# A step pipeline of hyperbolic attention: the chain from vector addition to feed-forward drawn together, its wide products on other steps

## The chip, the cores and the metric

One core of a Trainium2 chip runs the whole program. The time is device microseconds (us) of one execution; engines are PE (TensorE), DVE (VectorE), ACT (ScalarE), POOL (GpSimd) and SP, which issues the DMAs here.

## The reference, cut to what matters

The program is four blocks in a row on x of 8 samples, 512 rows, 256 columns, all in float32: a mixture of experts with a recurrent attention, a transformer block on the Poincaré ball, and two layers of windowed attention. The change touches the second alone. In this block `logmap0`, `expmap0` and `plin` scale each row by a function of its norm:

```python
ada = t_emb @ w_ada + b_ada
sh_msa, sc_msa, g_msa, sh_mlp, sc_mlp, g_mlp = jnp.split(ada, 6, axis=-1)
residual = x
xn = layer_norm(logmap0(x))
xm = expmap0(xn * (1 + sc_msa) + sh_msa)
...
attn = jax.nn.softmax(scores, axis=-1)
out_h = expmap0(jnp.einsum('bhqk,bhkd->bhqd', attn, vt))
attn_out = plin(_from_heads(out_h), w_o, b_o)
attn_t = g_msa * logmap0(attn_out)
x = mobius_add(residual, expmap0(attn_t))
residual = x
xn = layer_norm(logmap0(x))
xm = expmap0(xn * (1 + sc_mlp) + sh_mlp)
ff = plin(plin(xm, w_f1, b_f1), w_f2, b_f2)
ff_t = g_mlp * logmap0(ff)
return mobius_add(residual, expmap0(ff_t))
```

D is 256, there are 16 heads of 16, and the feed-forward is 1024 wide. `mobius_add` is the vector addition of the title.

## The kernel before, in words

`ball_parts` writes the block as a pipeline of numbered steps G. Each engine has a function `step(G)` that issues its share of step G, and each engine runs its steps in order; between the engines there are only semaphores. A sample has S = 16 attention steps (4 groups of heads times 4 key tiles), sample b those from 16b to 16b + 15, and everything else of a sample stands at a fixed distance from 16b: `at(G, 24)` gives the sample b with G = 16b + 24. What is due at distance a falls into the attention steps of a later sample, at phase a mod 16. A period is 16 steps; "phase 8" means the steps with G mod 16 = 8.

One step on PE is: the scores of step G + 1 (L1793), the side jobs of this step, the values of step G (L1806). ACT takes the exponentials of step G + 1 first (L1250, L1251, two halves of 1024 columns), then its other jobs. The scores use one set of four PSUM banks, so that those of G + 2 wait for the exponentials of G + 1.

The side jobs put their products into a ring of three PSUM banks (`RING`, `claim`, `place`): a job takes the bank that the job three places ahead of it had, and waits until ACT or DVE has emptied that one. The order of the ring is that of the jobs in the program. The jobs, with those who empty them:

- every fourth step: "ur" (the turned rows of the next sample's tile, L1848, emptied by ACT), phases 3, 7, 11, 15; "qk" and "v" (L1857, emptied on DVE by `projected`, L1449) and "pk" (row sums of the softmax, L1816, emptied by `invert`, L1503, at the end of the DVE step), phases 0, 4, 8, 12; "bc" (reciprocals spread, L1823, emptied by `divide`, L1514, near the start of the DVE step after), phases 1, 5, 9, 13; "zq" and "zk" (heads turned, L1841, emptied by ACT L1310 and by `keys`, L1493), phases 2, 6, 10, 14;
- once a sample: "wo0", "wo1" (product with w_o, L1832, emptied by `update` at the step after and by squares on ACT, L1269 to L1273), distances 18, 19; "fu0", "fu1" (rows of the feed-forward turned, L1865); "f0" to "f7" (first product of the feed-forward, two a step by the table `F1`, L1876, emptied by `hidden`, L1650); "fn" (norms, L1883); "y0" to "y3" (second product by `F2`, L1892, emptied one step later, `YS`, by `output_rows`, L1666).

On DVE the chain of a sample after its attention is: `update`, `step_limit`, `step_length`, `step_factors` (the first Möbius addition's factors), `applied` (L1564, the rows after ACT has scaled them in `scaled_rows`, L1326), `row_norms` (L1575), `row_angles` (seventeen operations on 128x4 and a root asked from POOL, L1217), `row_variances` (after a logarithm on ACT, L1354), `row_scales`, `rows2` (four tiles, into `u2`, which lies on the same memory as `fsq`, the squares of the hidden rows, so that it waits for POOL's sums of the sample ahead, `acc_ok`), `ask_rows2`, `limit_rows2`, then on ACT `scaled_rows2` and on PE "fu". A second chain of the same kind follows the outputs: `step_limit`, `step_length`, `step_factors`, `scaled_update` (ACT), `result`. `ask_heads` (L1457 and sixteen operations more) stands in phases 1, 5, 9 and 13, at the end of the DVE step, `limit_heads` (L1030 to L1484) at the start of phases 0, 4, 8 and 12.

The last sample has its attention in steps 112 to 127. All that comes after step 127 has no attention beside it; I call it the tail. The windowed layers are a block of their own and load their rows after the last result is stored.

## Time and profile before

| | us |
|---|---|
| median of 3 runs (lowest, highest) | 3677.0 (3676.5, 3677.7) |
| profiled execution, its own time | 3681.4 |
| its span | 3679.6 |
| PE busy in the span | 3405.7 (93%) |
| DVE busy | 2207.2 (60%) |
| ACT busy | 1698.4 (46%) |
| POOL busy | 383.3 (10%) |
| scores of step 0 of the ball block to scores of step 127 | 1230.5 to 2006.9 |
| scores of step 127 to the start of the windowed block | 2006.9 to 2155.0 |

Busy time says where an engine had work, not who waited: in this block the start of each group of scores on PE dates the steps, and the rows further down are windows cut at those starts. PE's clock is given there as a share of 2.4 GHz: 1.00 is 2.4 GHz, and 0.5 is 1.2 GHz.

### The profile page before, as it was taken

What the parts mean: (1) busy time and instruction counts of PE and PEld (TensorE: products, weight loads), DVE (VectorE), ACT (ScalarE), POOL (GpSimd) and SP (SyncE); (2) the same over time, 40 slices, a digit from 0 to 9 for tenths busy, and PEclk for the clock granted to TensorE, in tenths of its full rate; (3) what the DMA queues carried; (4) which work ended last, traced back from release to release, by engine and by line L of the source; (5) the groups of instructions that cost most, each with busy time, mean ns of one, the idle gap of its engine ahead of it and who ended that gap; (6) DMA issues with size and microseconds to landing.
All of it is one profiled execution on the core that took longest, in us unless ns stands there. A gap on an engine that the chain in (4) does not pass through costs nothing. (4 is left out here: it accounts for less than half of the span.)

```text
span 3679.6 us, 51595 instructions
## 1 busy us (share of the span) xinstructions
PE 3405.7 (93%) x18082; PEld 1915.6 (52%) x18082; DVE 2207.2 (60%) x6620; ACT 1698.4 (46%) x3271; POOL 383.3 (10%) x250
## 2 busy tenths in 40 slices
PE   8999999999996788998899758999999999999999
PEld 3455555555554333444444435555555555555554
DVE  3243343343357567778775648777777777777773
ACT  2233333333342455555556325555555555555552
POOL 0000000000000001111211211111111111111110
PEclk8999999999998799999999879999999999999999
DMA  4110120110000200000000030000000000000000
GB/s 175 53 61 32 35 72 32 35 61 32 29 15 13 76 5 8 7 15 14 11 12 12 9 131 21 20 21 21 21 21 21 21 27 21 26 27 27 21 27 20
DMA packets 77985, 120.47 MB, mean 33 GB/s; under 512 B 10224, under 2 KB 66315, under 8 KB 72608
## 3 DMA queue, kind: packets, MB, share of 16 engines
q1 hardware_dynamic: 77728, 117.17, 9.4%
q8 instruction: 146, 2.39, 0.3%
q14 instruction: 111, 0.91, 0.1%
HBM read 96.13 MB, written 16.83 MB: 31 GB/s over the span
## 5 line engine op out<-in xcount | busy, mean ns | idle before, releaser
L2616 PE MATMUL wps<-w_wqkv,w_hT 128*128 128x512 f32 x768 | 379.2, 618 | 3.1 <-DMA w_wo<-in_wwo 3.1
L2654 PE MATMUL wps<-w_xnT,w_w 128*128 128x512 f32 (+1 forms) x768 | 352.5, 599 | 24.5 <-DVE w_xnT L2479 20.3
L2238 POOL TENSOR_TENSOR w_rn<-w_n,w_mhalf 128x16 f32<-128x16 f32 x64 | 187.3, 2926 | 1097.7 <-DVE w_n L2416 1097.7
L2266 ACT ACTIVATE w_pr<-w_sm,w_nmx,w_rn 128x256 f32<-128x256 f32 (+1 forms) x512 | 286.5, 562 | 10.0 <-DVE w_nmx L2397 9.4
L1217 POOL TENSOR_TENSOR b_routs<-b_rins,b_expo 128x4 f32<-128x4 f32 x88 | 89.8, 1023 | 1839.0 <-DVE b_rins L1405 1839.0
L2654 PEld LDWEIGHTS wps<-w_xnT,w_w 128*128 128x128 f32 (+1 forms) x768 | 133.6, 179 | 217.9 <-issue 194.3
L656 PE MATMUL ps<-xT,b_late 128*128 128x512 f32 x512 | 245.8, 602 | 0.0
L672 PE MATMUL ps<-hid,b_late 128*128 128x512 f32 x512 | 240.8, 592 | 0.0
L1250 ACT ACTIVATE bb_pr<-ps 128x1024 f32<-128x1024 f32 x128 | 130.6, 1020 | 198.6 <-PE ps L1793 197.7
L2253 ACT ACTIVATE w_pT<-wps 128x512 f32<-128x512 f32 (+1 forms) x128 | 69.6, 544 | 329.7 <-PE wps L2563 329.7
L2616 PEld LDWEIGHTS wps<-w_wqkv,w_hT 128*128 128x128 f32 x768 | 138.2, 193 | 132.8 <-issue 127.8
L2666 PE MATMUL wps<-w_w,w_h2T 128*128 128x256 f32 (+1 forms) x768 | 190.1, 392 | 1.8 <-issue 1.8
L298 ACT ACTIVATE hid<-ps,rb 128x512 f32<-128x512 f32 x128 | 87.9, 687 | 222.6 <-PE ps L656 222.4
L2392 DVE CUSTOM_DVE_ANT_0 w_sm<-wps,w_wmask 128x256 f32<-128x256 f32 (+1 forms) x512 | 168.9, 386 | 34.8 <-issue 33.6
L2666 PEld LDWEIGHTS wps<-w_w,w_h2T 128*128 128x128 f32 (+1 forms) x768 | 137.4, 189 | 61.9 <-issue 48.6
L1876 PE MATMUL ps<-bb_uT,bb_wf 128*128 128x512 f32 x256 | 139.1, 689 | 31.8 <-DVE bb_fT L1650 14.4
L672 PEld LDWEIGHTS ps<-hid,b_late 128*128 128x128 f32 x512 | 97.1, 190 | 121.9 <-issue 121.5
L510 DVE TENSOR_REDUCE mx<-ps 128x8 f32<-128x512 f32 x32 | 22.1, 691 | 217.4 <-PE ps L753 217.4
L2275 ACT ACTIVATE w_qkr<-wps 128x512 f32<-128x512 f32 x128 | 76.4, 597 | 157.9 <-PE wps L2616 157.4
L2563 PEld LDWEIGHTS wps<-w_ident,w_pr 128*128 128x128 f32 x896 | 101.7, 142 | 77.0 <-issue 52.1
L407 DVE TENSOR_TENSOR hid<-hid,wm 128x512 f32<-128x512 f32 x128 | 88.3, 691 | 88.7 <-ACT hid L298 87.7
L2407 DVE TENSOR_SCALAR w_pr<-w_pr,w_ri 128x256 f32<-128x256 f32 (+1 forms) x512 | 137.6, 332 | 4.5
(329 smaller groups left out, 6680.4 us busy)
## 6 DMA issues: line engine op xcount, KB each, us to landing
b_late<-in_ew SPq DMA_DIRECT2D x32, 1024.0 KB, 6.7
w_xa<-xs SPq DMA_DIRECT2D x16, 512.0 KB, 3.9
w_xin<-xs SPq DMA_DIRECT2D x64, 128.0 KB, 3.8
xT<-in_xT SPq DMA_DIRECT2D x8, 512.0 KB, 3.8
xres<-in_x SPq DMA_DIRECT2D x32, 128.0 KB, 2.2
x<-x1t SPq DMA_DIRECT2D x32, 128.0 KB, 1.7
b_mod<-ada SPq DMA_DIRECT2D x16, 256.0 KB, 3.2
xs<-bb_wb SPq DMA_DIRECT2D x8, 512.0 KB, 2.9
```

The costliest lines, as they stand in the source:

```text
L656: ins = te.matmul(ps[:, G % 2], w1[:, k, j % M1 * P:(j % M1 + 1) * P], xT[:, b % 2, k], start=(k == 0), stop=(k == KD - 1))
L672: ins = te.matmul(ps[:, 2 + c], w2[:, j % M1, c * P:(c + 1) * P], hid[:, G % 4], start=(j == 0), stop=(j == J - 1))
L1250: a.activation(pr[:, G % 2, 0:2], ps[:, SC:SC + 2], ACT.Exp, scale=DH ** -0.5).then_inc(p_ok, 1)
L1876: ins = te.matmul(to, wf1[:, k, m * P:(m + 1) * P], uT2[:, k], start=(k == 0), stop=(k == KD - 1))
L2238: g.tensor_tensor(rn[:, i % 2, t], n2[:, n % 2, 1], mhalf[:], ALU.pow).then_inc(nr_ok, 1)
L2266: ins = a.activation(pr[:, j, lo:], sm[:, j, lo:], ACT.Exp, bias=nmx[:, G % 2, j:j + 1], scale=rn[:, i % 2, t, h:h + 1], accum_out=rs[:, G ...
L2392: ins = v.tensor_tensor_reduce(out=sm[:, j, lo:], in0=ps[:, g, c2 * 256 + lo:c2 * 256 + 256], in1=wmask[:, lo:], scale=1.0, scalar=-3.0e38 ...
L2407: ins = v.tensor_scalar(pr[:, j, lo:], pr[:, j, lo:], ri[:, G % 2, j:j + 1], None, ALU.mult)
L2563: ins = te.transpose(ps[:, 2 + g, (2 * c2 + k) * P:(2 * c2 + k + 1) * P], pr[:, j, k * P:(k + 1) * P], ident[:])
L2616: ins = te.matmul(to, hT[:, i % 2, k, t * P:(t + 1) * P], wqkv[:, i // B, k, s * 512:(s + 1) * 512], start=(k == 0), stop=(k == KD - 1))
L2654: ins = te.matmul(to[0:n], w1[:, i // B, k, lo:lo + n], xnT[:, k], start=(k == 0), stop=(k == KD - 1))
L2666: ins = te.matmul(to[:, a * D:(a + 1) * D], h2T[0:n, m, t * P:(t + 1) * P], w2[0:n, i // B, m], start=(m == 0), stop=(m == MH - 1))
```

## The change

Only distances and places within a step are changed; no operation is added or removed. By distance from 16b:

| job | before | after |
|---|---|---|
| first addition: `scaled_rows` (ACT), `applied` and `row_norms` | 24, 25 | 23, 24 |
| `row_angles` | 26 | 24, late in the DVE step |
| logarithm, `row_variances`, `row_scales` | 26, 27, 28 | 25, 25, 26 |
| `rows2` | 28, 29 | 26, 27 |
| `ask_rows2`, `limit_rows2`, `scaled_rows2`, "fu" | 31, 32, 32, 33 | 28, 28, 29, 30 |
| `F1` (two products a step) | 37, 39, 41, 43 | 31, 33, 37, 38 |
| "fn", `F2` | 45; 45, 46, 47, 49 | 41; 41, 42, 43, 45 |
| second chain: n1, `step_limit`, `step_length`, `step_factors` | 51, 52, 53, 54 | 47, 48, 49, 50 |
| `scaled_update`, `result`, store | 55, 56, 56 | 50, 51, 51 |

`row_angles` and `limit_rows2` moved down in the DVE step, behind `projected`; `scaled_rows` and `scaled_update` to the end of the ACT step, behind the logarithm. The core of the diff:

```diff
-    STEPS = range(-LEAD - 10, S * (B - 1) + 60)
-    F1 = {37: (0, 1), 39: (2, 3), 41: (4, 5), 43: (6, 7)}
-    F2 = {45: 0, 46: 1, 47: 2, 49: 3}
-    YS = {46: 0, 47: 1, 48: 2, 50: 3}
+    STEPS = range(-LEAD - 10, S * (B - 1) + 52)
+    F1 = {31: (0, 1), 33: (2, 3), 37: (4, 5), 38: (6, 7)}
+    F2 = {41: 0, 42: 1, 43: 2, 45: 3}
+    YS = {42: 0, 43: 1, 44: 2, 46: 3}
...
-            if at(G, 24) is not None:
-                scaled_rows(at(G, 24))
-            if at(G, 32) is not None:
-                scaled_rows2(at(G, 32))
-            if at(G, 55) is not None:
-                scaled_update(at(G, 55))
+            if at(G, 29) is not None:
+                scaled_rows2(at(G, 29))
...
+            if at(G, 23) is not None:
+                scaled_rows(at(G, 23))
+            if at(G, 50) is not None:
+                scaled_update(at(G, 50))
+            if at(G, 49) is not None:
+                hyperbolic(at(G, 49), th2_ask, th2_ok)
...
+            if at(G, 24) is not None:
+                applied(at(G, 24))
+                row_norms("r1", at(G, 24))
             if at(G, 25) is not None:
-                applied(at(G, 25))
-                row_norms("r1", at(G, 25))
+                row_variances("r2", "r", at(G, 25))
             if at(G, 26) is not None:
-                row_angles("r1", at(G, 26))
...
             if tile_due(G, 1) is not None:
                 projected(tile_due(G, 1))
+            if at(G, 24) is not None:
+                row_angles("r1", at(G, 24))
+            if at(G, 28) is not None:
+                limit_rows2(at(G, 28))
```

**DVE, phases 8 and 9 of a full period.** Before, phase 8 ends with `result` of an older sample, the rows of the next one, `projected` and `invert`, and `applied` opens phase 9:

```order
L1484 SCALAR_TENSOR_TENSOR b_late<-b_y,b_hf 128x16x16
L1683 SCALAR_TENSOR_TENSOR bb_wb<-bb_xb,b_cols,bb_wb 128x256 x4
L1429 SCALAR_TENSOR_TENSOR b_late<-bb_xb,b_mv,b_mod 128x256
L1431 SCALAR_TENSOR_TENSOR b_late<-b_late,b_cols,b_mod 128x256
L1449 SCALAR_TENSOR_TENSOR b_y<-ps,b_lim,b_bqkv 128x512
L1452 SCALAR_TENSOR_TENSOR b_y<-ps,b_lim,b_bqkv 128x256
L1503 RECIPROCAL bb_rcp<-ps 128x16
L1507 COPY bb_rcx<-bb_rcp 128x512
L1564 SCALAR_TENSOR_TENSOR bb_xb<-bb_wa,b_cols,bb_xb 128x256 x4
```

After the change `applied` and `row_norms` stand in phase 8, ahead of the same rows and of `projected`; `row_angles` (L1030 and on) follows before `invert`:

```order
L1564 SCALAR_TENSOR_TENSOR bb_xb<-bb_wa,b_cols,bb_xb 128x256 x4
L1415 MEMSET b_carrier 128x1
L1575 BN_STATS b_st<-bb_xb 128x6 x4
L1415 MEMSET b_carrier 128x1
L1579 BN_AGGR b_mv<-b_st 128x2 x4
L1035 TENSOR_TENSOR b_cols<-b_mv 128x4
L1035 TENSOR_TENSOR b_cols<-b_cols,b_mv 128x4
L1030 TENSOR_SCALAR b_cols<-b_cols 128x4
L1405 TENSOR_SCALAR b_rins<-b_cols 128x4
L1429 SCALAR_TENSOR_TENSOR b_late<-bb_xb,b_mv,b_mod 128x256
L1431 SCALAR_TENSOR_TENSOR b_late<-b_late,b_cols,b_mod 128x256
L1449 SCALAR_TENSOR_TENSOR b_y<-ps,b_lim,b_bqkv 128x512
```

So the DVE step of phase 8 lost `result` and got three jobs, two of them ahead of the emptying of "qk" and "v", all of them ahead of `invert`.

**PE, phases 5 to 7.** Before, with the first pair of `F1` (L1876) at phase 5 and the second at phase 7 behind "ur":

```order
L1876 MATMUL ps<-bb_uT,bb_wf 128x512 x4
L1823 MATMUL ps<-b_ident,bb_rcx 128x128 x4
L1806 MATMUL ps<-bb_pr,bb_val 32x512 x4
L1793 MATMUL ps<-bb_qT,bb_kT 128x512 x4
L1841 MATMUL ps<-b_ident,b_late 128x128 x8
L1806 MATMUL ps<-bb_pr,bb_val 32x512 x4
L1793 MATMUL ps<-bb_qT,bb_kT 128x512 x4
L1848 MATMUL ps<-b_ident,b_late 128x128 x2
L1876 MATMUL ps<-bb_uT,bb_wf 128x512 x4
```

After, with the third pair at phase 5 and the fourth at phase 6 behind the turned heads (L1841); phase 7 has "ur" alone:

```order
L1876 MATMUL ps<-bb_uT,bb_wf 128x512 x4
L1823 MATMUL ps<-b_ident,bb_rcx 128x128 x4
L1806 MATMUL ps<-bb_pr,bb_val 32x512 x4
L1793 MATMUL ps<-bb_qT,bb_kT 128x512 x4
L1841 MATMUL ps<-b_ident,b_late 128x128 x8
L1876 MATMUL ps<-bb_uT,bb_wf 128x512 x4
L1806 MATMUL ps<-bb_pr,bb_val 32x512 x4
L1793 MATMUL ps<-bb_qT,bb_kT 128x512 x4
```

**ACT, phases 2 and 3.** Before, the squares of an output tile stand ahead of the logarithm (L1354), and nothing stands between it and the table load of the next exponentials (L1250):

```order
L1310 ACTIVATE b_late<-ps 128x4x128
L1288 ACTIVATE b_junk,b_cols<-bb_ya 128x256
L1290 ACTIVATE b_junk,b_cols<-bb_wb 128x256
L1354 ACT_TABLE_LOAD
L1354 ACTIVATE b_cols<-b_cols 128x4
L1250 ACT_TABLE_LOAD
L1250 ACTIVATE bb_pr<-ps 128x1024
L1251 ACTIVATE bb_pr<-ps 128x1024
L1296 ACTIVATE b_uT<-ps 128x256
```

After the change `scaled_update` (L1326, on `bb_wb`) stands between, and waits for `step_factors` of the same DVE step:

```order
L1310 ACTIVATE b_late<-ps 128x4x128
L1354 ACT_TABLE_LOAD
L1354 ACTIVATE b_cols<-b_cols 128x4
L1326 ACTIVATE bb_wb<-bb_wb,b_cols 128x256 x4
L1250 ACT_TABLE_LOAD
L1250 ACTIVATE bb_pr<-ps 128x1024
L1251 ACTIVATE bb_pr<-ps 128x1024
L1296 ACTIVATE b_uT<-ps 128x256
L1269 ACTIVATE b_junk,b_cols<-ps 128x256
L1273 ACTIVATE b_junk,b_cols<-bb_wa 128x256
```

The load for L1250 and the exponentials of phase 3 now stand behind these four.

## Rows read from the trace of the kernel before

**Rows 1.** Windows, one per period of sixteen steps; the last is the tail. Length, busy, clock.

```profile
core 0: us, PE busy (x) PEld busy (x) DVE busy (x) ACT busy (x) POOL busy (x), PEclk, DMA share, GB/s
...
1309.40:1399.80 90.40, 72.42 (x408) 32.44 (x409) 64.76 (x244) 50.63 (x87) 7.02 (x7) 0.87 0.03 8
1399.80:1502.40 102.60, 90.30 (x488) 44.32 (x488) 79.28 (x265) 58.34 (x104) 19.50 (x18) 0.95 0.02 8
...
1718.80:1826.70 107.90, 97.69 (x524) 49.89 (x520) 86.86 (x304) 62.51 (x121) 20.53 (x19) 0.95 0.04 11
1826.70:1931.60 104.90, 97.73 (x514) 50.39 (x511) 70.29 (x236) 57.29 (x108) 17.57 (x16) 0.92 0.03 11
...
2006.90:2155.00 148.10, 98.62 (x344) 66.20 (x340) 75.43 (x256) 42.54 (x123) 33.33 (x30) 0.82 0.04 13
```

**Rows 2.** Windows, one per step of the fourth full period: phases 5, 7 and 9.

```profile
1756.80:1762.90 6.10, 6.10 (x32) 2.38 (x28) 3.85 (x14) 4.20 (x8) 1.01 (x1) 1.00 0.00 0
...
1766.10:1776.20 10.10, 7.73 (x28) 2.61 (x28) 8.22 (x40) 2.94 (x7) 0.00 (x0) 0.83 0.00 1
...
1781.80:1793.00 11.20, 7.89 (x32) 3.02 (x28) 10.87 (x35) 5.22 (x11) 1.57 (x3) 0.85 0.13 47
```

**Rows 3.** Timeline, PE, phase 7: start, length, operation, idle before it and releaser.

```profile
1769.22 0.62 PE L1848 MATMUL ps<-b_ident,b_late 128*128 128x128 f32 x2 [1.97 <-DVE bb_oT L1514]
1769.63 5.17 PE L1876 MATMUL ps<-bb_uT,bb_wf 128*128 128x512 f32 x8
```

**Rows 4.** Timeline, DVE, first operation of each job in phases 1 to 9.

```profile
1734.20 0.95 DVE L1457 TENSOR_REDUCE b_hn<-b_ysq 128x48 f32<-128x768 f32 x1 [0.47 <-ACT b_ysq L1303]
...
1738.31 0.69 DVE L1514 TENSOR_TENSOR bb_oT<-bb_raw,ps 128x512 f32<-128x512 f32 x1
...
1740.36 0.17 DVE L1030 TENSOR_SCALAR b_cols<-b_routs 128x4 f32<-128x4 f32 x1
...
1743.88 0.69 DVE L1493 COPY b_late<-ps 128x512 f32<-128x512 f32 x1
...
1750.52 0.69 DVE L1499 COPY bb_raw<-ps 128x512 f32<-128x512 f32 x1 [2.87 <-PE ps L1806]
...
1752.73 0.68 DVE L1521 TENSOR_TENSOR bb_wa<-ps,bb_gate 128x512 f32<-128x512 f32 x1
...
1755.18 0.75 DVE L1449 SCALAR_TENSOR_TENSOR b_y<-ps,b_lim,b_bqkv 128x512 f32<-128x512 f32 x1
...
1756.86 0.16 DVE L1405 TENSOR_SCALAR b_rins<-b_cols 128x4 f32<-128x4 f32 x1
...
1762.92 0.94 DVE L1457 TENSOR_REDUCE b_hn<-b_ysq 128x48 f32<-128x768 f32 x1
...
1768.39 0.69 DVE L1514 TENSOR_TENSOR bb_oT<-bb_raw,ps 128x512 f32<-128x512 f32 x1
...
1787.15 1.66 DVE L1564 SCALAR_TENSOR_TENSOR bb_xb<-bb_wa,b_cols,bb_xb 128x256 f32<-128x256 f32 x4
...
1791.46 1.40 DVE L1650 TENSOR_SCALAR bb_fT<-ps,bb_bf 128x512 f32<-128x512 f32 x2
```

**Rows 5.** Timeline, ACT, change of table between phases 2 and 3.

```profile
1744.67 1.28 ACT L1250 ACT_TABLE_LOAD   x1 [1.46 <-PE ps L1806]
1745.96 1.02 ACT L1250 ACTIVATE bb_pr<-ps 128x1024 f32<-128x1024 f32 x1
```

**Rows 6.** Timeline, PE, tail after the last scores.

```profile
2021.64 1.80 PE L1865 MATMUL ps<-b_ident,bb_fsq 128*128 128x128 f32 x8 [2.41 <-ACT bb_fsq L1326]
...
2029.09 7.17 PE L1832 MATMUL ps<-bb_wo,bb_oT 128*128 128x256 f32 x32 [0.78 <-DVE bb_oT L1514]
...
2051.39 5.97 PE L1876 MATMUL ps<-bb_uT,bb_wf 128*128 128x512 f32 x8 [6.45 <-DVE bb_fT L1650]
...
2091.16 1.97 PE L1865 MATMUL ps<-b_ident,bb_fsq 128*128 128x128 f32 x8 [3.71 <-ACT bb_fsq L1326]
...
2098.37 5.31 PE L1876 MATMUL ps<-bb_uT,bb_wf 128*128 128x512 f32 x12
```

101 lines of the change are left out of this document (47 added, 54 removed).

## The prediction

> **What bounds the kernel now.** The page first: PE is busy 93% of the span, DVE 60%, and the chain that ended last says only that the windowed layers end the program. The change lies in the ball block, so I cut that block into periods. In a full period [rows 1] the 16 steps take 107.9 us; PE is busy 97.7 and DVE 86.9 of them, and DVE's work is not spread evenly. A step's own products do not need that time: phase 5, with a pair of `F1` products and "bc", takes 6.1 us with PE never idle, while phase 7 with such a pair takes 10.1 and phase 9 takes 11.2, at clocks of 0.83 and 0.85 [rows 2]. In phase 7 "ur" wants the bank that "bc" had, waits 1.97 us for `divide`, and the pair behind it then takes 5.17 us: after that idle time PE is granted its lower level, 1.2 GHz, for part of it [rows 3]. DVE is late there because `ask_heads`, with `divide` behind it, ran until 1768.39, over 5 us behind the start of PE's step [rows 4]. So a full period is PE's work plus what PE waits for banks that DVE empties late. Adding what each step needs without a wait gives about 93 us, 15 less than measured. Behind step 127 comes a tail of 148.1 us with PE busy 98.6 of it at a mean clock of 0.82 [rows 1]: a chain, not a load.
>
> **The prices** [rows 4], first row of a job to first row of the next: `ask_heads` 4.1 us (1734.20 to 1738.31), but 5.5 (1762.92 to 1768.39) where POOL sums hidden squares at the same time; `row_angles` 3.5; `take` with `limit_heads` 2.2; `projected` with `invert` 1.7; `applied` with `row_norms` 4.3; `hidden` 0.66 for each product; `divide` 0.6. `step_factors` is thirteen operations of the kind of `row_angles`, 2.5 by its spacing of 0.2. On PE, from the 6.1 us of phase 5 [rows 2]: about 1.1 each for scores and values, 3.5 for a pair of `F1`, 0.6 for "bc"; a "wo" or "y" tile is 3.5 too, half of the 7.17 in [rows 6].
>
> **A full period after the change, step by step.** No operation is added, so DVE still needs about 88 us a period; what counts is where. I walk PE and DVE through the steps from the start of phase 0, with the ring's order at hand.
> Phase 1 now has f2, f3 and "bc" and ends at 11.7. DVE can empty f3 only at 11.0 and then does `ask_heads` until 15.8, so `divide` is done at 16.4; "wo0" is ready to run at 14.1 and waits 2.4. Phase 2 ends at 21.0, against 7.2 us for the step now.
> In the same DVE step follow `row_angles` and `step_factors`, until 22.4. ACT has `scaled_update` at the end of its step, waits for those factors, needs 1.7 for the four rows, then loads its table (1.28, and the exponential begins at once [rows 5]) and has the exponentials of phase 3 only at 27.3; the squares that empty "wo0" and "wo1" follow. Phase 4 ends at 34.3, 1 us or 2 later than by PE's own work.
> In phase 5 DVE must wait for f4 and f5 and then has `ask_heads` with POOL beside it: until 45.8. Phase 6 now has f6 and f7, and f6 wants the bank of "bc": PE idles 3.8 us there, from 42.6 to 46.4. Phase 6 ends at 51.0 and phase 7, with "ur" alone, at 54.2.
> Phase 8 on DVE is `take`, `limit_heads`, `applied`, `row_norms`, rows, `projected`, `row_angles`, `invert`: 2.2 + 4.3 + 0.95 + 3.5 + 1.7 = 12.6 us. PE's phase 9 idles 1.5 before "fn" and has "bc" at the end of it, at 67. DVE goes on with `row_variances` and `ask_heads` to 73 and only then empties y0, whose bank "zk" wants: 3.8 us idle in phase 10, which ends at 79.2. Phases 11 to 15 have light DVE steps and need their own 29 us. Sum: 108.2 us at the higher clock. As in phase 7 now, an idle time of some 2 to 4 us may be followed by products at 1.2 GHz, 1.5 to 1.7 us each (5.17 in [rows 3] against 3.5 for a pair); two of the three long waits lead straight into products on the path. Bounds: 108.2 with none, 112 with both and a late ACT. I take 110.3, since such a wait is followed by it more often than not. That is +2.4 for each of the three full periods, +7.
> So the spread does not buy what it seems to: the pairs left phases 7, 9 and 11, but the waits moved to phases 2, 6, 9 and 10.
>
> **The other periods** [rows 1]. In the first one with a chain (90.4 us) there are no `F1` products yet; the chain ends sooner on DVE: -2. The next (102.6) gets the full load of PE but no second chain on DVE: about 108.5, +6. The one from 1826.7 (104.9) loses the heads and rows of the next sample on DVE, but not the waits in phases 6 and 10: about 106.5, +1.5. The last stays within 1: +1. Before step 23 nothing changes. Together +6.5, with the full periods +13.5.
>
> **The tail** [rows 6]. After step 127 there is no attention, so distances count only as order. Now: "fu" of the seventh sample at 2021.64, "wo" of the eighth at 2029.09, then all four pairs of the seventh sample's `F1` beside the eighth's chain; PE waits 6.45 us for DVE at 2051.39, the eighth's "fu" comes at 2091.16, and a "y" of the seventh still stands between it and the eighth's `F1` at 2098.37. After: the seventh's "fu" and first pair run in steps 126 and 127 in place of two "y" tiles, so "wo" starts at about 2022 if step 127 were as early, -7. From the end of "wo" (now 2036.3) to the eighth's `F1` it takes 62 us now. After, DVE has in front of it only one chain, two pairs and three outputs: update 1.5, squares 1.1, four small jobs 1.5, factors 2.5, `applied` and `row_norms` 4.3, angles 3.5, variances 1.6, scales and `rows2` 4, limits 0.5, the rows scaled on ACT twice 3.5, five roots with their way to POOL and back at 1.1 less what lies beside other work 4.5, four hidden tiles 2.6, three outputs 4.3, 0.6 for "fn", and 2.7 for "fu" and its emptying; sum 38.7, with POOL in the way 40. Gain 22. From the eighth's `F1` to 2155 nothing changes: the second chain of the seventh stands beside the eighth's pairs as it does now. Tail: -29; bounds -20 (a wait for a "y" or for POOL left over) and -34. The start of the windowed block, its loads and its clock move along with it.
>
> **Sum.** 3681.4 + 13.5 - 29 = 3666 for an execution such as the profiled one, which was 4.4 above the median of the runs; against the median 3661.5.
>
> **A rule of the skill beside it.** The rows show 1.28 us for a table load and the exponential 0.01 us behind it [rows 5]; the sum goes by that. The Trainium skill (ScalarE: Activation LUTs, What ACT_TABLE_LOAD costs) puts a switch at 2.66 us, a drain of 1.38 included. By that rule the load that the change put behind `scaled_update` would hold the exponentials of phase 3 for another 1.4 us, in three periods: 4 us more, 3666. This trace does not show the drain.
> The rows of `ask_heads` say 4.1 us alone and 5.5 beside POOL [rows 4]. I gave phase 1 4.8, since only the second of two sums falls on it. The Trainium skill (SBUF — State Buffer, Who interferes with whom) calls the port pair of VectorE and GpSimd an exclusive lock; by that rule phase 1 could cost the whole 1.4, 0.7 more a period, 3 us in all.
>
> **Rivals.**
> A. *As walked* (chance 0.55): 3661, within 3650 to 3669.
> B. *The spread works* (0.17): DVE catches up sooner than I let it, the waits in phases 2, 6 and 10 shrink to a microsecond each, and the periods come down toward the 93 us of PE's own work, to about 102. For it: PE's sum by steps is even now. Against it: DVE's 88 us leave little to catch up with, and it must wait for f3 and f5 before its longest job. Five periods at -6 and the tail: 3620 to 3650, about 3635.
> C. *The waits grow into the clock and ACT* (0.13), the side of slower. Place: phases 2 to 4 and 6. ACT gets its factors 2 us later than walked, the exponentials of phase 3 come behind the scores' need, and all three long waits are followed by 1.2 GHz. Price 4 to 5 us more a period than walked, 115 against 107.9, four periods and a fifth in part: +22 on A, 3684, about +0.2%. It decides from a period above 114.
> D. *The change does not shorten the tail* (0.15): in the last period, or by a bank that is still held, the seventh sample's pairs are as late as now, and only 10 to 15 us are gained: 3672 to 3682, no change.
>
> **How the numbers follow.** A measurement of this kernel can tell about 0.2%, 7.4 us, so that faster is below 3669.7 and slower above 3684.4. Faster: A nearly whole (0.53), B (0.17), little of D: 0.72. Slower: half of C and a little of errors beyond it: 0.10. The rest is 0.18. The range takes A, D, the lower half of C and the upper half of B: 3641 to 3682.
>
> **What the profile after would show.** Steps 0 to 22 as before. Full periods of 108 to 112 us, with phases 7 and 11 short (3.2 and 6), phase 6 at 9 to 12 and phase 10 at 9 to 12 with PE idle before L1876 and L1841 until DVE L1514 and L1666, and some 2 us before L1832 in phase 2. The tail near 119 us, the eighth sample's "fu" about 40 us behind the end of its "wo". Periods below 105 would say B; a tail over 130, D; a period over 114, C. If the periods grow and the tail shrinks by amounts that do not match these, the sum may be right by luck, and then it is wrong.

## The result, and the profile after

| | before | after the change |
|---|---|---|
| median, 4 runs each | 3677.34 us | 3704.11 us (3703.09 to 3707.28) |
| ratio | 1 | 1.0074, 95% interval 1.0060 to 1.0088 |
| span of the profiled execution | 3679.6 us | 3705.5 us |
| scores of step 127 begin at | 2006.9 us | 2059.2 us |
| from there to the windowed block's first product | 155.2 us | 132.6 us |

The change makes the kernel 0.74% slower, 27 us, where 3661 (3641 to 3682) was forecast. The steps with attention end 52.3 us later, the tail is 22.6 us shorter. What is behind the tail is the same program and took 3.8 us less in this execution (1513.7 against 1517.5 us); over all the runs below it lies between 1513.1 and 1517.5, whatever the version. The same windows as [rows 1] with the same columns, of the kernel after; the third has no counterpart there, the sixth is the tail:

```profile
1311.20:1407.90 96.70, 75.43 (x416) 33.92 (x416) 65.73 (x247) 52.68 (x92) 8.21 (x8) 0.85 0.03 8
1407.90:1522.70 114.80, 99.95 (x527) 52.50 (x524) 81.48 (x278) 61.18 (x116) 18.69 (x17) 0.93 0.03 7
1522.70:1639.00 116.30, 99.38 (x524) 52.98 (x520) 86.51 (x303) 62.98 (x122) 20.88 (x19) 0.94 0.04 12
1755.00:1871.10 116.10, 100.82 (x526) 53.49 (x523) 86.39 (x303) 63.04 (x122) 20.86 (x19) 0.93 0.04 10
1871.10:1979.40 108.30, 93.57 (x515) 48.69 (x511) 71.51 (x236) 57.67 (x109) 17.62 (x17) 0.97 0.04 11
2059.20:2184.70 125.50, 85.23 (x296) 55.13 (x292) 69.85 (x239) 38.13 (x107) 32.06 (x30) 0.82 0.04 15
```

| period from step | -1 | 15 | 31 | 47 | 63 | 79 | 95 | 111 |
|---|---|---|---|---|---|---|---|---|
| before, us | 78.9 | 90.5 | 102.6 | 108.2 | 108.2 | 107.9 | 104.9 | 75.3 |
| after, us | 79.5 | 96.8 | 114.8 | 116.3 | 116.0 | 116.1 | 108.3 | 79.8 |
| forecast of the difference | 0 | -2 | +6 | +2.4 | +2.4 | +2.4 | +1.5 | +1 |
| measured | +0.6 | +6.3 | +12.2 | +8.1 | +7.8 | +8.2 | +3.4 | +4.5 |

The last full period against the one of [rows 1]: DVE has as much to do as before (86.4 us against 86.9), PE is busy 3 us more for the same products, which is its clock (0.93 against 0.95), and is idle 5 us more (15.3 against 10.2). Step by step, for the period that begins with phase 15 (from the starts of the scores):

| phase | 15 | 0 | 1 | 2 | 3 | 4 | 5 | 6 | 7 | 8 | 9 | 10 | 11 | 12 | 13 | 14 |
|---|---|---|---|---|---|---|---|---|---|---|---|---|---|---|---|---|
| before | 5.9 | 5.6 | 7.0 | 7.2 | 5.9 | 6.4 | 6.1 | 3.2 | 10.1 | 5.6 | 11.2 | 3.2 | 10.1 | 5.6 | 7.4 | 7.4 |
| after | 5.9 | 5.6 | 6.1 | 11.5 | 5.9 | 6.4 | 6.1 | 14.5 | 3.2 | 5.6 | 12.7 | 7.7 | 5.9 | 5.6 | 6.2 | 7.1 |

The windows of phases 2, 6, 9, 10 and 14, with the granted clock in the third place from the end:

```profile
1772.60:1784.10 11.50, 8.43 (x44) 5.46 (x40) 10.02 (x47) 4.39 (x7) 1.55 (x2) 0.85 0.00 0
1802.60:1817.10 14.50, 9.79 (x36) 3.85 (x33) 9.92 (x26) 3.85 (x9) 4.78 (x4) 0.76 0.00 0
1825.90:1838.60 12.70, 10.20 (x48) 7.30 (x44) 11.28 (x57) 4.55 (x7) 4.15 (x4) 0.73 0.00 0
1838.60:1846.40 7.80, 6.89 (x48) 4.29 (x44) 6.93 (x21) 5.54 (x12) 0.00 (x0) 1.00 0.01 2
1864.00:1871.10 7.10, 4.23 (x38) 2.19 (x35) 6.29 (x22) 3.77 (x8) 0.00 (x0) 1.00 0.09 12
```

PE's timeline in them: start, length, operation, idle before it and releaser.

```profile
1777.87 5.38 PE L1832 MATMUL ps<-bb_wo,bb_oT 128*128 128x256 f32 x16 [3.07 <-DVE bb_oT L1514]
...
1803.67 1.09 PE L1841 MATMUL ps<-b_ident,b_late 128*128 128x128 f32 x8
1809.47 6.71 PE L1876 MATMUL ps<-bb_uT,bb_wf 128*128 128x512 f32 x8 [4.71 <-DVE bb_oT L1514]
...
1829.57 1.84 PE L1883 MATMUL ps<-b_ones,bb_acc 128*128 128x1 f32 x8 [2.50 <-DVE b_y L1449]
1831.27 6.05 PE L1892 MATMUL ps<-bb_wf,bb_fT 128*128 128x256 f32 x16
...
1868.63 0.66 PE L1841 MATMUL ps<-b_ident,b_late 128*128 128x128 f32 x4 [2.87 <-DVE bb_ya L1666]
```

Before wo0 PE waits 3.07 us, before f6 4.71, before "fn" 2.50, before "zk" of phase 14 2.87. The products behind the first three run in part at 1.2 GHz: wo0 takes 5.38 us where half of the 7.17 in [rows 6] is 3.6, the pair of f6 and f7 6.71 where such a pair takes 3.70 at 2.4 GHz (below), y0 6.05. Phases 2, 6 and 9 have granted clocks of 0.85, 0.76 and 0.73. What PE waits for in phase 6 stands in DVE's timeline:

```profile
1801.27 0.75 DVE L1650 TENSOR_SCALAR bb_fT<-ps,bb_bf 128x512 f32<-128x512 f32 x1 [0.97 <-PE ps L1876]
...
1802.61 0.94 DVE L1457 TENSOR_REDUCE b_hn<-b_ysq 128x48 f32<-128x768 f32 x1
...
1803.82 1.25 DVE L1030 TENSOR_SCALAR b_rinh<-b_hn 128x51 f32<-128x51 f32 x1
...
1805.33 1.15 DVE L1032 TENSOR_SCALAR b_routh<-b_routh 128x51 int32<-128x51 int32 x1
...
1808.73 0.69 DVE L1514 TENSOR_TENSOR bb_oT<-bb_raw,ps 128x512 f32<-128x512 f32 x1
```

PE is through with "zq" and "zk" at 1804.76 and could then run f6; DVE empties f5 until 1802.02, does `ask_heads` from 1802.61 and reaches `divide` at 1808.73. This is the kind of wait that [rows 3] and [rows 4] show for phase 7 before, with more of the wide products behind it.

### The profile page after: what moved, and what is told of

The parts are those of the page before. It is cut to its first block and busy times, and to the rows that moved or that the text cites. A ratio compares the mean times of both kernels' runs of the same rounds, so it can differ in the third digit from the quotient of the medians.

```text
span 3705.5 us, 51595 instructions
## 1 busy us (share of the span) xinstructions
PE 3412.5 (92%) x18082; PEld 1926.7 (52%) x18082; DVE 2207.4 (60%) x6620; ACT 1702.1 (46%) x3271; POOL 384.6 (10%) x250
## 5 line engine op out<-in xcount | busy, mean ns | idle before, releaser
L1217 POOL TENSOR_TENSOR b_routs<-b_rins,b_expo 128x4 f32<-128x4 f32 x88 | 91.1, 1040 | 1825.6 <-DVE b_rins L1405 1825.6
L1250 ACT ACTIVATE bb_pr<-ps 128x1024 f32<-128x1024 f32 x128 | 130.8, 1022 | 187.6 <-PE ps L1793 187.1
L1876 PE MATMUL ps<-bb_uT,bb_wf 128*128 128x512 f32 x256 | 133.4, 671 | 30.7 <-DVE bb_oT L1514 23.5
L2275 ACT ACTIVATE w_qkr<-wps 128x512 f32<-128x512 f32 x128 | 76.5, 597 | 155.3 <-PE wps L2616 155.0
```

What stands on the lines that cost most here:

```text
L1250: a.activation(pr[:, G % 2, 0:2], ps[:, SC:SC + 2], ACT.Exp, scale=DH ** -0.5).then_inc(p_ok, 1)
L1876: ins = te.matmul(to, wf1[:, k, m * P:(m + 1) * P], uT2[:, k], start=(k == 0), stop=(k == KD - 1))
```

## The experiments

Each is compared with runs of the kernel before on the same chip (medians 3674.0 to 3677.8). "Full periods" is the mean length of the three full periods in its profile (the periods from steps 47, 63 and 79); the changed kernel has 116.0 to 116.3, the one before 107.9 to 108.2.

| run | time, us | ratio to before (95%) | full periods, us | tail to the windowed block, us |
|---|---|---|---|---|
| after the change | 3704.1 | 1.0074 (1.0060 to 1.0088) | 116.1 | 132.6 |
| e_late_only | 3682.7 | 1.0018 (1.0009 to 1.0027) | 108.1 | 133.3 |
| e_heads_later | 3642.1 | 0.9913 (0.9900 to 0.9927) | 109.4 | 132.9 |
| e_before_heads | 3646.0 | 0.9923 (0.9909 to 0.9936) | 109.3 | 155.3 |
| e_act_order | 3701.7 | 1.0080 (1.0066 to 1.0094) | 114.0 | 132.9 |
| e_f67_later | 3698.0 | 1.0062 (1.0048 to 1.0076) | 114.5 | 130.0 |
| e_filler | 3744.2 | 1.0188 (1.0174 to 1.0202) | 121.0 | 134.5 |
| e_filler4 | 3708.5 | 1.0089 (1.0073 to 1.0104) | 114.3 | 133.3 |
| e_chain_behind | 3724.1 | 1.0127 (1.0112 to 1.0143) | 117.4 | 131.3 |
| e_heads_chain_behind | 3650.6 | 0.9930 (0.9916 to 0.9943) | 111.5 | 133.4 |
| e_wide_later | 3781.1 | 1.0288 (1.0274 to 1.0302) | 126.9 | 146.0 |
| e_heads_wide_later | 3703.0 | 1.0073 (1.0060 to 1.0087) | 116.1 | 145.7 |
| e_first_chain_old | 3737.5 | 1.0168 (1.0154 to 1.0181) | 119.3 | 143.0 |
| e_second_chain_old | 3718.5 | 1.0115 (1.0099 to 1.0130) | 117.9 | 136.6 |
| e_heads_result_later | 3639.4 | 0.9904 (0.9888 to 0.9919) | 107.1 | 135.0 |
| e_heads_ahead_of_hidden | 3643.0 | 0.9906 (0.9891 to 0.9921) | 108.5 | 134.6 |

### Is the tail a gain of its own?

e_late_only gives each distance one value for the early samples and one for the late: e2(G, old, new) is the sample that is due by the old distance if it is one of the first five, by the new one if not.

```diff
-            if at(G, 41) is not None:
-                ask_hidden(at(G, 41))
+            if e2(G, 45, 41) is not None:
+                ask_hidden(e2(G, 45, 41))
...
+    F1_MID = {34: (0, 1), 35: (2, 3), 37: (4, 5), 38: (6, 7)}
```

(The lines are picked from a longer diff and not in its order; `F1_MID` is the sixth sample's.)

> Samples 1 to 5 keep every distance of the kernel before, the sixth keeps the old first chain but has the second half of the new plan, the seventh and eighth have the new distances throughout. Theory W (the full periods are where the change loses, and the shorter tail is a gain of its own): the stretch up to the scores of step 127 stays within 0 to 5 us of before (before 2006.9 us from the span's start, after the change 2059.2), the tail is about 125 us as after the change against 148 before, so 3655 to 3661 us. Rival T (the tail is short only because the earlier periods were stretched, work of the seventh sample being done by then): the tail stays near 140 to 148, so 3669 to 3680 us.

```profile
1930.60:2034.90 104.30, 94.05 (x470) 50.29 (x467) 51.24 (x175) 53.27 (x108) 18.08 (x16) 0.87 0.03 11
2034.90:2161.10 126.20, 84.72 (x296) 54.74 (x292) 69.81 (x238) 38.10 (x107) 32.04 (x30) 0.82 0.05 15
```

The full periods are those of before (108.2, 108.0 and 108.0 us) and the tail is as short as after the change (126.2 against 125.5 us in the same window), so the full periods have no part in it. By itself that does not refute Rival T: the one period just ahead of the tail is stretched, by more than the tail gains. The next two runs settle it. e_heads_later and e_before_heads take 179.3 and 177.0 us for the last two periods with attention, and their tails are 132.9 and 155.3 us: 22.4 us less behind a stretch that is only 2.3 us longer. The time of e_late_only is not W's, by my own transition: the period before the tail takes 104.3 us in place of 75.3. The sixth sample's pairs had to be out of the way of the seventh's `rows2` and crowd into four steps with "wo0" and "wo1" (phase 3 alone takes 15.3 us); +29 and -22 leave +0.2%.

### ask_heads ahead of the divides

```diff
-            if tile_due(G, 2) is not None:
-                ask_heads(tile_due(G, 2))
+            if tile_due(G, 3) is not None:
+                ask_heads(tile_due(G, 3))
```

> The changed kernel with VectorE's ask_heads (4.1 to 5.5 us) moved from the end of the steps of phases 1, 5, 9, 13 to the end of the steps behind them, so behind the divide, the output_rows and the hidden copies of those steps. Theory W (TensorE waits 3.1, 4.7, 0.9 and 2.9 us in phases 2, 6, 10 and 14 for a divide or an output that stands behind ask_heads, and its clock falls to 1.2 GHz behind those waits): these waits go or fall below 1 us, the 6.8 us stretch at 1.2 GHz in phase 6 goes, the full periods fall from 116 to 104 to 109 us, 3664 to 3682 us. Rival P (the bunched products themselves, more work than a step has room for, set the length, and the waits only show it): full periods at 113 or more, 3692 us or more.

> The kernel before (not the changed one) with the same single move of ask_heads as in e_heads_later, which took the changed kernel from about 3704 to 3642 us. Theory H (what ask_heads costs is its own matter, and the wide products stand as badly with it gone): before gains as much or more, its full periods fall to 98 to 102 us and it ends at 3620 to 3640 us, below the changed kernel with the move. Rival I (the change was made worse by ask_heads alone; without it the new plan is the better one): before gains 10 to 30 us only, 3646 to 3667 us, and the changed kernel with the move is the faster of the two by 5 us or more.

First e_heads_later, then e_before_heads; each the first period and the last full one:

```profile
1227.80:1292.80 65.00, 56.22 (x359) 22.42 (x359) 43.16 (x139) 41.58 (x55) 4.88 (x5) 0.95 0.30 104
...
1701.30:1810.60 109.30, 97.68 (x528) 51.14 (x524) 86.25 (x304) 62.95 (x121) 20.85 (x19) 0.94 0.04 10
```

```profile
1224.50:1292.80 68.30, 59.56 (x360) 23.58 (x360) 43.29 (x139) 41.58 (x55) 4.80 (x5) 0.90 0.28 99
...
1688.30:1797.50 109.20, 100.66 (x524) 52.65 (x520) 87.30 (x304) 62.71 (x121) 20.51 (x19) 0.92 0.03 11
```

One call moved by a step gives the changed kernel 62 us and the kernel before 30. In the changed kernel phase 2 falls from 11.5 to 6.5 us, phase 6 from 14.5 to 6.6, phase 14 from 7.1 to 5.3, while phases 4 and 8, where other waits come up, grow from 6.4 to 11.0 and from 5.6 to 9.6; the first period with heads only (79.5) falls to 65.0 although nothing of the change is in it. The waits that Theory W named go; the full periods (109.4) end at the upper edge of its range, and its time was named 22 us too high, because I had priced the full periods and not those ahead, which give 14.5, 13.4 and 8.7 us. Before gains 30 us, the upper end of Rival I and less than half of what Theory H asks for, all of it outside its full periods, which do not fall (109.3). In the last of them phases 7, 9 and 11 shrink by 9.6 us together, but phases 8 and 13 grow from 5.6 and 7.4 to 11.2 and 13.1, behind two other waits:

```profile
1747.39 2.04 PE L1857 MATMUL ps<-b_wqkv,b_uT 128*128 128x256 f32 x4 [2.76 <-DVE bb_fT L1650]
...
1782.34 1.84 PE L1883 MATMUL ps<-b_ones,bb_acc 128*128 128x1 f32 x8 [3.29 <-DVE b_y L1449]
```

"v" waits for a hidden copy, which now stands behind `ask_heads` on DVE, and "fn" for `projected`. So with ask_heads out of the way the full periods of the two plans are equally long, for different reasons, and the changed plan is the faster by 4 us (3642.1 against 3646.0, about 0.1%, less than a measurement tells). By the traces it is 22.4 us less in the tail, 4.5 more in the last period with attention and 7.6 more in the others, so 10 less; what lies ahead of step -1 and behind the tail, where nothing was changed, differs by 3 us each between these two executions, as it does between others. The change costs 27 us where ask_heads stands ahead of the divides and nothing that can be told from zero where it does not: its loss is its meeting with ask_heads. This is Rival I but for its margin of 5 us.

What is left in e_heads_later:

```profile
1739.42 1.17 PE L1816 MATMUL ps<-bb_pick,bb_raw 128*128 128x4 f32 x8 [3.97 <-ACT b_junk L1271]
...
1765.11 1.05 PE L1816 MATMUL ps<-bb_pick,bb_raw 128*128 128x4 f32 x8 [2.31 <-DVE bb_raw L1499]
...
1768.46 2.09 PE L1793 MATMUL ps<-bb_qT,bb_kT 32*128 32x512 f32 x8 [1.30 <-ACT bb_pr L1251]
1772.69 1.84 PE L1883 MATMUL ps<-b_ones,bb_acc 128*128 128x1 f32 x8 [2.14 <-DVE b_y L1449]
1774.39 5.33 PE L1892 MATMUL ps<-bb_wf,bb_fT 128*128 128x256 f32 x16
```

PE waits 3.97 us in phase 4 for the squares that empty wo1, and three times in phases 8 and 9. The granted clock is at 1.2 GHz for 10.2 us from 1767.47 on, so from the second of these three waits until y0 (the scores behind it take 2.09 us in place of 1.14).

```diff
-            if at(G, 51) is not None:
-                result(at(G, 51))
+            if at(G, 53) is not None:
+                result(at(G, 53))
```

> e_heads_later with result and the store two steps later (53 in place of 51: phase 5, where VectorE sat idle 3.4 us, in place of phase 3). Theory Q (in phases 2 to 4 VectorE is busy without a gap from ask_heads to update, and TensorE's wait of 4.0 us in phase 4 is for wo1's bank behind it): the wait falls by result's 1.7 us to 2 to 2.5 us, periods 107 to 108.5 us, 3636 to 3641 us. Rival R (that wait is not on VectorE's order): periods within 0.5 us of 109.3, 3641 to 3645 us.

The wait in phase 4 falls to 2.4 us, two of the three full periods to 106.3 and 106.4 and one to 108.5, and the time to 3639.4: as Theory Q has it. It has the lowest time of all, 1.0% below the kernel before (0.9888 to 0.9919); from e_heads_later and e_heads_ahead_of_hidden the intervals do not tell it.

### The clock

```diff
+            if at(G, 38) is not None and attends(G + 1):
+                pe.wait_ge(p_ok, 2 * G + 4)
+                for r in range(12):
+                    te.matmul(ps[:, SC + r % 4], ident[:], wf1[:, 0, 0:L], start=True, stop=True)
```

> The changed kernel with 12 matmuls of 128x512 whose results nobody reads, put on TensorE in phase 6 ahead of f6 and f7, once the step's scores have been read by ScalarE: they fill some 2.6 us of the 4.7 us in which TensorE waits there for the divide. Theory K (the wait itself is not longer than before, and half of phase 6's 14.5 us is the clock: f6, f7 and the values run at 1.2 GHz for 6.8 us): the granted clock stays at 2.4 GHz, phase 6 falls to 10 to 12 us, 3690 to 3698 us. Rival L (the clock falls all the same, or DVE's end sets the phase): phase 6 stays at 14 to 17 us and the time at 3702 to 3712 us.

Phase 6 grew to 18.1 us and the time to 3744.2, beyond both ranges, since I had priced the fillers wrongly: a matmul of these shapes is two passes and 0.86 us, twelve are 10.3 us, over 5 more than the wait. f6 and f7 did run at 2.4 GHz. So the number was changed:

```diff
-                for r in range(12):
+                for r in range(4):
```

> e_filler with 4 matmuls in place of 12. There each took 0.86 us of TensorE (two passes of 0.43 us), 10.3 us in all and so 5 us more than the wait it was to fill, phase 6 grew to 18.1 us, but f6 and f7 ran at 2.4 GHz, 3.5 us for the pair in place of 6.7. Four take 3.4 us of the 4.7 us wait. Theory K (the low clock behind the wait is a cost of its own of 3 us in each period): the pair takes 3.5 us, phase 6 falls from 14.5 to 11 to 12 us, 3691 to 3698 us. Rival L (the filled wait comes back as a later one): the pair is fast but the periods stay within 1 us of 116, 3701 to 3706 us.

PE in phase 6 with four fillers (L1917), to be held against 4.71 us idle and 6.71 above:

```profile
1797.52 3.70 PE L1917 MATMUL ps<-bb_wf,b_ident 128*128 128x512 f32 x8 [1.03 <-ACT bb_pr L1251]
1801.18 3.70 PE L1876 MATMUL ps<-bb_uT,bb_wf 128*128 128x512 f32 x8
```

f6 and f7 take 3.70 us, phase 6 11.5, with a granted clock of 1.00: 3 us of phase 6's 14.5 were the clock and not the wait. Full periods fall by 1.8 us only (114.1 to 114.5), since low-clock stretches come up elsewhere (phase 3 or 15), and step 118, where nothing waited, now takes 11.3 us in place of 5.7. The whole is as slow as the change (3708.5, the intervals overlap). Theory K holds for the phase; the time is Rival L's kind, though 2.5 us above its range, and the periods fell by more than the 1 us that it allows.

### Single steps of the change

In ScalarE's step, against the changed kernel:

```diff
-            if at(G, 29) is not None:
-                scaled_rows2(at(G, 29))
...
                 queries(tile_due(G, 7))
+            if at(G, 29) is not None:
+                scaled_rows2(at(G, 29))
```

> The changed kernel with ScalarE's scaled_rows2 put behind head_squares and queries in its step (phase 13) instead of ahead of them. Theory W (VectorE waits 5.2 us for head_squares there, and TensorE 2.9 us in phase 14 behind it): phase 14's wait goes, 2 to 3 us less in each of four or five periods, 3690 to 3697 us. Rival G (the wait is given back in the next steps, since something else of that stretch ends as late): within 3 us of the changed kernel, 3701 to 3706 us.

What VectorE waited for after the change, in phase 13:

```profile
1863.38 0.95 DVE L1457 TENSOR_REDUCE b_hn<-b_ysq 128x48 f32<-128x768 f32 x1 [5.17 <-ACT b_ysq L1303]
```

Phase 14 falls from 7.1 to 5.5 us (its wait from 2.87 to 1.3), the full periods by 1.4 to 3.1 us; the time, 2.4 us below the change's, is not to be told from it (the ratios to before are 1.0080 and 1.0074). By the time that is Rival G; of Theory W half holds, in the phase. VectorE's 5.17 us for `head_squares`, which the forecast had overlooked, were real, but only half of PE's wait hung on them.

```diff
-    F1 = {31: (0, 1), 33: (2, 3), 37: (4, 5), 38: (6, 7)}
+    F1 = {31: (0, 1), 33: (2, 3), 37: (4, 5), 39: (6, 7)}
```

> The changed kernel with the products f6 and f7 moved one step, from phase 6 (beside zq and zk, 14.5 us) to phase 7 (beside ur alone, 3.2 us). Theory W (they wait in phase 6 for the divide behind ask_heads and run at 1.2 GHz; a step later the divide is long done): phase 6 falls to 6 to 8 us and phase 7 rises to 7 to 9, full periods 110 to 113 us, 3688 to 3697 us. Rival G (the squares' chain to fn in phase 9 gets as much longer, or the wait and the low clock go along to phase 7): full periods 115 to 117 us, 3700 to 3708 us.

Phases 6 and 7 together fall from 17.7 to 13.1 or 13.4 us: in phase 7 PE waits 2.6 us before "ur", with the low clock behind it, as the kernel before does. Phase 9 grows from 12.7 to 14.6, its wait before "fn" from 2.5 to 4.5. Of the 4.5 us two thirds are given back, as Rival G has it in kind; the full periods (114.5) and the time (3698.0) lie between the two ranges, and by the ratios (1.0062 and 1.0074) the run is not to be told from the change.

```diff
-            if at(G, 24) is not None:
-                applied(at(G, 24))
-                row_norms("r1", at(G, 24))
...
             if tile_due(G, 1) is not None:
                 projected(tile_due(G, 1))
+            if at(G, 24) is not None:
+                applied(at(G, 24))
+                row_norms("r1", at(G, 24))
```

and `invert` ahead of `row_angles` in that step.

> The changed kernel with VectorE's step of phase 8 in another order: projected, applied and row_norms, invert, row_angles in place of applied, row_norms, projected, row_angles, invert. Theory M (the chain that was drawn in to phase 8 stands ahead of the tile's projected there and holds fn in phase 9 by 2.5 us, behind which the clock is at 1.2 GHz for 6.8 us): the wait before fn goes, phase 9 falls from 12.7 to 8 to 10 us, 3688 to 3697 us. Rival N (VectorE has as much to do in phases 8 and 9 in any order, and the wait only moves to bc of phase 9 or to phase 10): periods within 2 us of 116, 3698 to 3706 us.

PE in phases 9 and 10:

```profile
1836.68 1.05 PE L1885 MATMUL ps<-b_ones,bb_acc 128*128 128x1 f32 x8
1837.59 3.70 PE L1894 MATMUL ps<-bb_wf,bb_fT 128*128 128x256 f32 x16
...
1846.14 0.63 PE L1843 MATMUL ps<-b_ident,b_late 128*128 128x128 f32 x4 [2.35 <-DVE b_lim L1654]
1851.74 1.11 PE L1843 MATMUL ps<-b_ident,b_late 128*128 128x128 f32 x4 [4.97 <-DVE bb_ya L1666]
```

"fn" no longer waits and phase 9 falls to 7.0 us, but phase 10 now waits 2.35 and 4.97 us for `ask_hidden` and the output of y0, and takes 15.5 us in place of 7.7. It is Rival N's mechanism, with a loss I had not named: 20 us, beyond both ranges. The work is the same in any order; what is put last is late.

> e_heads_later (3642 us) and e_chain_behind in one kernel. If the two causes (ask_heads ahead of the divides, the drawn-in chain ahead of projected) are separate, the gains add: full periods of 104 to 107 us in place of 109.3, 3626 to 3636 us. If the long low-clock stretch over phases 8 to 10 (10.2 us in e_heads_later) comes from the waits of 2.3 and 1.3 us in phase 8 rather than from fn's wait, it stays, and the time is 3636 to 3643 us.

3650.6 us is beyond both: periods of 110.4 to 112.7, 8.5 us worse than e_heads_later. The second cause gains nothing in this form, with or without the first.

### Parts put back

The wide products, with fn, limit_hidden and the second chain two steps later too:

```diff
-    F1 = {31: (0, 1), 33: (2, 3), 37: (4, 5), 38: (6, 7)}
-    F2 = {41: 0, 42: 1, 43: 2, 45: 3}
-    YS = {42: 0, 43: 1, 44: 2, 46: 3}
+    F1 = {35: (0, 1), 37: (2, 3), 39: (4, 5), 41: (6, 7)}
+    F2 = {43: 0, 44: 1, 45: 2, 47: 3}
+    YS = {44: 0, 45: 1, 46: 2, 48: 3}
```

> The changed kernel with the first chain (up to fu) as drawn in, and the wide products at one pair every second step again: f pairs at distances 35, 37, 39, 41 (phases 3, 5, 7, 9), the second products at 43, 44, 45, 47, and what hangs on them two steps later than in the change. Theory S (it is the place of the wide products, one pair beside zq and zk in phase 6 above all, by which the change loses in the full periods): periods of 106 to 111 us, 3668 to 3685 us. Rival C (it is the first chain, whose VectorE work now stands in phases 8 to 12 ahead of the tile's own): periods of 114 to 118 us, 3698 to 3715 us.

> e_wide_later with ask_heads moved a step as in e_heads_later (which ended at 3642 us with full periods of 109.3). If the wide products' place matters only where ask_heads stands ahead of the divides, the full periods stay at 108 to 111 us and the time at 3640 to 3655 us; if the unbunched products are the better plan by themselves, periods are 103 to 107 us and the time 3622 to 3636 us.

The first lies beyond both theories, by 9 us a period from the nearer one: 126.3 to 127.4. With a pair in every second step, phases 2, 3, 4, 7, 9, 11 and 12 take 8 to 14 us each (before wo0, "qk", "ur" and f6 PE waits 3.5, 4.3, 2.6 and 4.4), and the tail is 13 us longer. With ask_heads moved, both expectations were missed as well: 116.1. So the crowding of the change (two pairs side by side in phases 5 and 6, none in 3, 7, 8 or 11) is not what it loses by: with the chain where it now is, this even spread is far worse, by 11 us a period, and by 7 with ask_heads moved. The runs do not part the pairs' places from those of the second products and the second chain, which moved two steps with them.

The first chain put back, with the pairs as near to the change's as it lets them be:

```diff
-    F1 = {31: (0, 1), 33: (2, 3), 37: (4, 5), 38: (6, 7)}
...
+    LATE1, LATE2 = 99, -1
...
+    F1_MID = {33: (0, 1), 35: (2, 3), 37: (4, 5), 38: (6, 7)}
...
-        if at(G, 30) is not None:
-            yield "fu0", at(G, 30)
-            yield "fu1", at(G, 30)
...
+        if e1(G, 33, 30) is not None:
+            yield "fu0", e1(G, 33, 30)
+            yield "fu1", e1(G, 33, 30)
```

(`e1` is to the first chain what `e2` is to the second half; with these two limits every sample takes the old distances of the first chain, `F1_MID`, and the new ones from "fn" on.)

> The changed kernel with its whole first chain back on the distances and places of the kernel before (scaled_rows 24 to scaled_rows2 32, fu 33), f pairs at 33, 35, 37, 38 (phases 1, 3, 5, 6), everything from fn on as in the change. Theory C (the first chain's VectorE work in phases 8 to 12 is what lengthens 9, 10 and 14): phases 9, 10 and 14 shrink by 3 us or more together, though f pairs now crowd phases 1 and 3; periods of 109 to 113 us, 3675 to 3692 us. Rival S (the crowded products cost as much or more; every plan that has f6 and f7 in phase 6 loses there): phase 6 stays at 13 to 15 us and periods at 115 us or more, 3698 us or more.

The 16 phases from phase 15 on, in us, from its trace: 3.2, 5.6, 9.5, 12.7, 9.5, 11.7, 6.1, 14.1, 3.2, 5.6, 7.0, 8.1, 5.9, 5.6, 6.5, 5.1. Phases 9, 10 and 14 shrink from 27.5 to 20.2 us together, Theory C's mechanism, though not its periods: the chain that was drawn in to phases 8 to 12 costs 7 us there. But "fu" at 33 pushes the pairs into phases 1 and 3, which with 2 and 4 grow by 13.5 (PE waits 2.3, 2.8 and 4.3 us), and the tail loses 10 of its 22 us. The period (119.3) and the time are Rival S's, and phase 6 stays at 14.

The second chain put back:

```diff
-            if at(G, 50) is not None:
-                step_factors(at(G, 50), th2_ok, fac2_ok)
-            if at(G, 51) is not None:
-                result(at(G, 51))
+            if at(G, 54) is not None:
+                step_factors(at(G, 54), th2_ok, fac2_ok)
+            if at(G, 56) is not None:
+                result(at(G, 56))
```

> The changed kernel with the second chain (n1 to result and store) back on the distances of before, 51 to 56 in place of 47 to 51, so in phases 3 to 8 in place of 15 to 3. Theory D (its step_length and step_factors in phases 1 and 2 add to what stands ahead of the divide of phase 2): the wait of 3.1 us in phase 2 falls by 1 to 2 us, but the chain's jobs now add 1.9 us to phases 5 and 6, where TensorE waits for VectorE as well, so periods of 114 to 117 us and 3698 to 3708 us. Rival E (the jobs are short and idle time of VectorE takes them anywhere): no phase changes by over 0.5 us, 3702 to 3706 us. The tail does not change in either, since its steps are empty (132 us).

The wait in phase 2 falls by 0.3 us only, and the wait before "fn" in phase 9 grows from 2.5 to 4.7: neither theory had the place right, and the periods of 117.9 are above D's. The tail is 4 us longer, where none was expected. The drawn-in second chain is worth 14 us to the change.

Last, against e_heads_result_later:

```diff
+            if tile_due(G, 3) is not None:
+                ask_heads(tile_due(G, 3))
             if among(G, F1):
                 for m in among(G, F1)[1]:
                     hidden(among(G, F1)[0], m)
             if tile_due(G, 1) is not None:
                 projected(tile_due(G, 1))
...
-            if tile_due(G, 3) is not None:
-                ask_heads(tile_due(G, 3))
```

> e_heads_result_later (3639 us) with ask_heads put ahead of the hidden copies in its step; that matters in phase 6 alone, where it ran 6.5 us behind f6's and f7's copies, beside GpSimd's sums of squares, against 3.8 to 4.1 us in the other phases. Theory F (the 2.4 us are contention with GpSimd and delay take in phase 8): ask_heads takes about 4.1 us in phase 6, the waits of 2.3 and 1.3 us in phase 8 shrink to 1 us together, periods fall by 2 to 4 us from 106.3 and 108.5, 3628 to 3636 us. Rival H (the contention moves to whatever VectorE does beside the sums, or f6's and f7's banks come free later and hold qk and v in phase 8): periods within 1.5 us, 3636 to 3643 us.

One correction first: the 6.5 us named there include the first operations of `step_factors`; `ask_heads` itself took 5.15 us (1755.81 to 1760.96). DVE of e_heads_ahead_of_hidden, and under it the sums of GpSimd:

```profile
1756.25 0.95 DVE L1457 TENSOR_REDUCE b_hn<-b_ysq 128x48 f32<-128x768 f32 x1
...
1760.35 1.41 DVE L1650 TENSOR_SCALAR bb_fT<-ps,bb_bf 128x512 f32<-128x512 f32 x2
1761.67 1.65 DVE L1035 TENSOR_TENSOR b_cols<-b_cols 128x4 f32<-128x4 f32 x3
1763.35 1.18 DVE L1032 TENSOR_SCALAR b_cols<-b_cols 128x4 f32<-128x4 f32 x1
```

```profile
1761.84 2.67 POOL L1228 TENSOR_TENSOR bb_acc<-bb_acc,bb_fsq 128x512 f32<-128x512 f32 x2 [7.17 <-ACT bb_fsq L1323]
```

`ask_heads` takes 4.1 us, as Theory F says, but the two sums now hold two operations of `step_factors`: three of L1035 take 1.65 us where they take 0.55, and one of L1032 takes 1.18 in place of 0.17. The contention goes along, as Rival H has it. The larger part of the story lies elsewhere. The waits of 2.3 and 1.3 us in phase 8 are gone, which is Theory F's, but in phase 7 a longer one has come up; ACT and PE:

```profile
1761.13 1.29 ACT L1323 ACTIVATE bb_fsq<-bb_fT 128x512 f32<-128x512 f32 x2 [4.17 <-DVE bb_fT L1650]
```

```profile
1764.30 2.09 PE L1793 MATMUL ps<-bb_qT,bb_kT 32*128 32x512 f32 x8 [4.36 <-ACT bb_pr L1251]
```

ACT squares the hidden rows ahead of the next exponentials, so it waits 4.17 us for the copies that now stand behind `ask_heads`, and PE waits 4.36 for those exponentials. Phase 7 grows from 3.2 to 6.9 us, phase 8 falls from 9.6 to 8.1, and the full periods grow by 1.4 us in the mean. The time of 3643.0 is at the upper edge of Rival H's range.

## Why the prediction was wrong

**The price list and what bounds the kernel.** Right in kind. The prices hold, a pair of `F1` excepted (3.70 us for 3.5). PE waits for banks that DVE empties late, and the phases that were named wait for the operations that were named: 2, 6, 9 and 10, with phase 7 at 3.2 and 11 at 5.9 us. Phase 6 is longer than the 9 to 12 us that were given (14.5), phase 10 shorter (7.7), with a wait of 0.91 us for 3.8.

**"I take 110.3": the step that failed.** The walk's 108.2 us have four waits of 2.4, 3.8, 1.5 and 3.8, 11.5 in all; measured are 3.07, 4.71, 2.50 and 0.91, and 2.87 in phase 14, 14.1 in all, so 2.6 us more. On them the forecast put 2.1 us for the clock, with 3.8 as its bound. Measured against 3.6 us for a "wo" or "y" tile and 3.70 for a pair, wo0 lost 1.8 us, y0 2.4 and the pair 3.0, 7.2 in all; e_filler4 shows the last by itself; "fn" lost 0.8 more. Set against each other term by term, the forecast has 96.7 us of PE's work, 11.5 of waits and 2.1 of clock, and the period of 116.1 has 92.8, 15.3 (with the small waits) and 8.0. So the clock term was 5.9 us too small and the waits 3.8, and the walk's work was 3.9 too large and hid that much of the error.

The clock's share was taken from one row of before, [rows 3], where 1.5 us were lost. The prediction's own figures held a larger one: 107.9 us less 10.2 idle [rows 1] less "about 93" of work leave 4.7 us for the clock, on waits of much the same total. And that one row was a matter of luck: in the period before it PE waited 1.97 us for `divide` in phase 7 as well, and the granted clock stayed at 1.00.

That this period should exceed 114 was Rival C, chance 0.13: its clock part is what happened, in all of the three long waits. Its other part is not: `scaled_update` did end late, but the exponentials of phase 3 began 25.9 us behind the start of phase 0, where the walk had 27.3 and Rival C 2 us more, and phases 3 and 4 took 5.9 and 6.4 us as before. Rival C's 3684 was still 20 us short. Rival B's price was added up wrongly: five periods at -6 and the tail's -29 are 3618 and not about 3635.

**"Phases 11 to 15 have light DVE steps."** The wait of phase 14 was not foreseen. ACT does `scaled_rows2` ahead of `head_squares` in phase 13; e_act_order puts half the wait on that.

**"ask_heads" beside POOL.** Right in kind, too small in phase 5's step: 4.8 was given to phase 1 (measured 5.06, 1771.98 to 1777.04) and 5.5 to phase 5's step (measured 6.12). Both sums fell into the latter, and each sum that holds an operation costs 1.0 us over the 4.1. The 0.7 us more that the rule set beside phase 1 came out at 0.26.

**"The chain ends sooner on DVE: -2", "+6".** Wrong by 8 and 6 us, 14 together, the largest error beside the full periods (17). In the first period with a chain many steps are short, six of the sixteen take 3.2 us before the change, and the distances count steps, so DVE's jobs of one step do not fit beside PE's: PE waited 4.9 us before "bc" in phase 9 for `invert`, which now stands behind `applied`, `row_norms` and `row_angles`. It waited 5.1 more before "fu" in phase 14, where before had no "fu", for the `divide` behind `ask_heads`, which itself waited 5.7 us for ACT's `head_squares` behind `scaled_rows2`. The second of the two periods has the waits of a full one (phase 6 takes 14.6 us and phase 9 12.8), so its 6 us are the failed step once more.

**The tail.** Rival D fell: the gain was 22.6 of the 29 us, within the bounds of 20 to 34 (125.5 us in the window for which 119 were forecast). PE in it:

```profile
2074.44 7.17 PE L1832 MATMUL ps<-bb_wo,bb_oT 128*128 128x256 f32 x32 [1.00 <-DVE bb_oT L1514]
...
2094.50 1.87 PE L1883 MATMUL ps<-b_ones,bb_acc 128*128 128x1 f32 x8 [6.02 <-POOL bb_acc L1228]
...
2108.70 8.86 PE L1892 MATMUL ps<-bb_wf,bb_fT 128*128 128x256 f32 x32 [2.35 <-DVE b_lim L1654]
2122.34 1.62 PE L1865 MATMUL ps<-b_ident,bb_fsq 128*128 128x128 f32 x8 [4.77 <-ACT bb_fsq L1326]
2124.84 14.95 PE L1876 MATMUL ps<-bb_uT,bb_wf 128*128 128x512 f32 x28 [0.89 <-issue]
2145.45 3.78 PE L1876 MATMUL ps<-bb_uT,bb_wf 128*128 128x512 f32 x4 [5.66 <-DVE bb_fT L1650]
```

"wo" starts 15.2 us behind the last scores, in place of 22.2: -7, as said. From the end of "wo" to the eighth's first pair it is 43.2 us, where 40 were worked out and 62 measured before. The rest of the error is in "from the eighth's `F1` nothing changes": there f7 waits 5.66 us for f4's copy, which DVE does behind the seventh sample's `result` (1.67 us at 2143.06, itself 1.77 us behind ACT's `scaled_update`), and the way to the windowed block is 67.0 us, 3.3 more than before.

**The rule on the table load.** By it phase 3's exponentials would have come 1.38 us later. ACT after the change:

```profile
1783.75 1.71 ACT L1326 ACTIVATE bb_wb<-bb_wb,b_cols 128x256 f32<-128x256 f32 x4 [4.69 <-DVE b_cols L1559]
1785.48 1.28 ACT L1250 ACT_TABLE_LOAD   x1
1786.77 1.02 ACT L1250 ACTIVATE bb_pr<-ps 128x1024 f32<-128x1024 f32 x1
```

The load begins 0.02 us behind `scaled_update` and the exponential 0.01 us behind the load: the drain that the Trainium skill (ScalarE: Activation LUTs, What ACT_TABLE_LOAD costs) adds is not seen here either, and the sum was right to leave it out.

**Sum.** Forecast +13.5 and -29, measured +52.3 and -22.6 (and -3.8 behind the tail, in one execution): the sign was lost in the periods. Of their 38.8 us of error, 17.1 are the three full periods, 14.5 the two ahead of them, the rest the two behind (5.4), the first one and the start.

What stays open: what decides whether the low clock follows a wait. Its length does not. A wait of 2.50 us in phase 9 is followed by it and one of 2.87 in phase 14 is not; the same wait before wo0 (3.07 and 3.06 us) comes with a clock of 0.85 in phase 2 of the changed kernel and of 1.00 in e_filler4's last full period; and the 2.87 us before "zk" in phase 14 come with 0.87 in e_f67_later. So from rows of single waits the forecast could not have placed the low stretches, only taken their share of a whole period. Open is also whether a version with before's distances for the first samples and the new ones for the last, with a transition that crowds nothing, keeps the 22 us whole. That was not tried.

## What to carry to other kernels

This pipeline by numbered steps was bound by the places where an in-order engine has something long and unhurried ahead of something short that others wait for. Look for that first and move the long one: one call by one step was worth 62 us here, more than all the distances, and it took away the whole loss of the change. But each such move brought up another wait, so walk the new order through before you move (e_chain_behind, e_heads_ahead_of_hidden). Price the clock behind the waits from whole periods, busy time and idle time apart, and not from the one row at hand; and walk the light periods by their own step lengths, since distances in steps shrink with them.

## What the runs showed of the hardware

**A sum on GpSimd holds at most one small VectorE operation, until it ends.** In phase 6 of the changed kernel two sums (2.68 us from 1803.75) fall on L1030 at 1803.82 (1.25 us) and L1032 at 1805.33 (1.15 us), which take 0.19 us elsewhere; each time about 1 us. Of the 56 such sums of 128x512 in its trace (L1228), 41 hold one operation for 0.2 to 1.1 us and none holds two, and each held operation ends 0.02 to 0.05 us behind the sum. Beside the other 15 VectorE had nothing to do (six), or a hidden copy (L1650), a `divide` (L1514) or the reduction of `ask_heads`, of which the first two read PSUM: these took their usual 0.75, 0.68 and 0.94 us. The 88 roots that POOL takes of 128x4 (L1217, 1.0 us each) hold nothing. In e_heads_later too a reduction of 128x768 that ran beside the start of a sum took 0.94 us as ever. That agrees with the Trainium skill (SBUF — State Buffer, Who interferes with whom): the port pair that the two engines share is an exclusive lock, `tensor_scalar` in its two-port modes and `tensor_tensor` with both inputs in SBUF can run into it, and `tensor_reduce` cannot. I had not expected it to be so regular: one sum, one held operation, whichever comes (e_heads_ahead_of_hidden).

**The clock can be held up by work.** Four matmuls that nobody reads, in the place of idle time, kept the granted clock of phase 6 at 1.00 in each full period, and brought the pair behind them from 6.71 to 3.70 us. It gained the kernel nothing (3708.5 against 3704.1 us), since the stretches at 1.2 GHz came up behind other waits.
